# A graph attention layer with residual and layer norm: the third tile's masks put first, x loaded by rows a quad at a time, an early flag, and the moments spread between mask steps

## The chip, the cores and the metric

The kernel runs on one core of a Trainium2 chip. The metric is device time in microseconds (us) of one execution. Engines are called PE (TensorE, the matrix engine; PEld is its weight load), DVE (VectorE), ACT (ScalarE), POOL (GpSimd) and SP (SyncE, here only a DMA queue). ACT and POOL also start DMAs from their own queues.

## What is computed

```python
f1 = (w1 @ (W @ x.T)).T + b1                 # 4096 x 1
f2 = (w2 @ (W @ x.T)).T + b2
logits = f1 + f2.T                           # 4096 x 4096
bias = where(adj > 0, 0, -1e9)
coefs = softmax(leaky_relu(logits) + bias, axis=-1)
y = x + coefs @ x                            # x is 4096 x 128, float32
out = (y - mean(y)) / sqrt(var(y) + 1e-5)    # over the 128 columns
```

adj is 4096 x 4096 int32 (64 MiB), so the whole matrix has to be read once.

## The kernel before

Leaky relu has two branches, and on each the exponential of f1 + f2 is a product of a row factor and a column factor. So `coefs @ x` is, for each row tile, two sums over columns: one with the mask "edge and f1 + f2 negative" (m = 1, called minus) against a table of x scaled by exp(0.01 f2), one with the mask "edge and positive" (m = 0, plus) against a table scaled by exp(f2). The tables `btv[m]` are 32 blocks of 128 columns; each block is 258 wide: x in float16 (high part), its denominator column, and a low part that restores precision. They are built in four chunks of eight blocks (h = 0 to 3): `scale_x` (DVE) or `scale_act`/`scale_first` (ACT) multiply x by the column factor, `split_x` (ACT) writes the high part, `low_x` (DVE) the low part.

The 4096 rows are 32 tiles of 128 rows, in 8 quads of four; a quad's tile c uses buffer slot c. Per tile: SP and ACT each load half of the 2 MiB of adj (`load_tile`, `load_far`); DVE makes int8 of it (`cast`, L743); ACT writes the sign of f1 + f2 in four instructions (`signs`, L474); DVE joins the two (`combine`, L748), transposes in 32 x 32 squares (`turn`, L756) and derives the plus mask (`plus`, L761); PE does 32 matmuls for minus and 32 for plus (`edge_sums`, L1091) of 258 columns each; ACT takes both sums out of PSUM scaled by the row factors (`evacuate`). `turn` of tile t waits until PE is done with tile t-4, whose mask buffers it overwrites.

Per quad, `moments(q - 2)` on DVE adds the sums, divides, adds x from `xn`, and takes mean and variance; POOL makes the reciprocal deviation (`rows`), ACT normalises, POOL stores. It stands in one block between the second and the third tile of quad q.

Ahead of the loop is a stage written out by hand, in which each engine's order is fixed. PE transposes x block by block (`turn_x`), ACT copies that out (`xT_out`), PE multiplies it with a vector to get f1 by columns (`f1_columns`, L1047); DVE gets f2 from products and row sums (`f2_products`, L693 and L697). `spread_f1` (L710) waits for the last `f1_columns`. `stat_max`/`stat_out` bring ranges of f1 and f2 to all partitions. The first four tiles are done in this stage, with the tables growing beside them. On POOL, seven small instructions compute the row factors' exponents (`ea`, from L385) and then ten more a flag (L396 to L409) that says whether the fast path is numerically safe; SP, ACT, POOL, PE and DVE read it before the loop. ACT's first signs in the loop (tile 4) come after that read. x in row order, `xn` (2 MiB, 512 bytes a row piece), is loaded by four DMAs of 512 KiB on POOL's queue (L380), after `f1_made` and the second cast.

Of the kernel before, what the change touches and what calls it, by code (L numbers as in the profile page):

```python
# [5 lines left out]
ALU = mybir.AluOpType  # L6
# [10 lines left out]
P = 128  # L17
# [25 lines left out]
def gat_kernel(nc, x, adj, W, w1, b1, w2, b2, out):  # L43
# [24 lines left out]
    with ExitStack() as ctx:  # L68
# [14 lines left out]
        junk = sb("junk", [P, KB * D], BF16)  # L83
# [70 lines left out]
        F2_PE = (0, 2)  # L154
        F2_AT = (FIRST * KB, NK - FIRST * KB)
# [6 lines left out]
        f2_made = sem("f2_made")  # L162
# [41 lines left out]
        y_act = sem("y_act")  # L204
        y_ready = [sem(f"y_ready{m}") for m in range(2)]
# [143 lines left out]
        def _(pool):  # L349
# [25 lines left out]


            pool.wait_ge(f1_made, 2)
# [6 lines left out]
            pool.wait_ge(gst_ready, 2)  # L384
# [11 lines left out]
            pool.tensor_tensor(rng[:, 0:1], gst[:, 0:1], gst[:, 1:2], ALU.add).then_inc(rng_step, 1)  # L396
            pool.tensor_scalar(rng[:, 1:2], gst[:, 0:1], gst[:, 1:2], None, ALU.max).then_inc(rng_step, 1)
            pool.wait_ge(rng_step, 2)
            pool.tensor_tensor(rng[:, 1:2], rng[:, 1:2], gst[:, 2:3], ALU.add).then_inc(rng_step, 1)
            pool.tensor_scalar(rng[:, 0:1], rng[:, 0:1], F2_SPAN, None, ALU.is_le).then_inc(rng_step, 1)  # L400
            pool.tensor_scalar(rng[:, 2:3], gst[:, 3:4], (SCALE * X_MAX) ** 2, None, ALU.is_le).then_inc(rng_step, 1)
            pool.tensor_scalar(rng[:, 3:4], gst[:, 3:4], (SCALE * X_MIN) ** 2 * N, None, ALU.is_ge).then_inc(rng_step, 1)
            pool.wait_ge(rng_step, 6)
            pool.tensor_scalar(rng[:, 1:2], rng[:, 1:2], F_ABS, None, ALU.is_le).then_inc(rng_step, 1)
            pool.tensor_tensor(rng[:, 2:3], rng[:, 2:3], rng[:, 3:4], ALU.mult).then_inc(rng_step, 1)
            pool.wait_ge(rng_step, 8)
            pool.tensor_tensor(rng[:, 0:1], rng[:, 0:1], rng[:, 1:2], ALU.mult).then_inc(rng_step, 1)
# [39 lines left out]
            with pool.Else():  # L447
                with pool.Fori(0, NT) as t:
# [8 lines left out]
        def _(act):  # L457
# [13 lines left out]
            def signs(t, c, between=None):  # L471

                for g in range(G):
                    ins = act.activation(sgn[:, c, g * JA:(g + 1) * JA], f2b[:, :], ACT.Sign,  # L474
                                         bias=nf1l[:, bass.ds(G * t + g, 1)], scale=-1.0)
                    if g == 1 and between:
                        between()
                ins.then_inc(sign_ready, 1)
# [6 lines left out]
            def f2_copy(i):  # L485

                b = F2_PE[i]
                bank, at = (0, F2_AT[0] + b * KB) if b < FIRST else (7, F2_AT[1] + (b - FIRST) * KB)
                act.wait_ge(f1_made if b < FIRST else f2_made, 1)
                act.activation(f2l[:, b * KB:(b + 1) * KB], ps[:, bank, at:at + KB], ACT.Copy).then_inc(f2l_act, 1)  # L490

            def f2_sums(n0, n1):
                act.wait_ge(xv_ready, 3)
                for n in range(n0, n1):
# [723 lines left out]
```

## Time and profile before

| | us |
|---|---|
| median of 3 runs | 274.12 (273.82 to 276.17) |
| the profiled execution | 275.19 |
| its span, first to last instruction | 273.5 |
| TensorE's mean granted clock | 0.997 |

The profile is of one execution. Its page gives for each engine the busy time and its share of the span; the same in 40 equal slices; the DMA queues; the chain of work that ended last; and the costliest groups of instructions. From the trace come the timeline (instructions in order of time), the waits, and busy time by windows. A releaser behind `<-` is what ended an idle time.

### The profile page before, as it was taken

To read this page: it belongs to the slowest core of one execution; us is meant where nothing else is said; L and a number is where in the kernel's file an instruction comes from. 1 tells how busy PE (TensorE), PEld (TensorE's weight loads), DVE (VectorE), ACT (ScalarE), POOL (GpSimd) and SP (SyncE) were. 2 spreads that over 40 slices of the span, in tenths; PEclk is the share of its full clock that TensorE was granted. 3 is DMA by queue.
4 is the path that set the end of the run, shared out by engine and by line. 5 is a ranking of instruction groups with operands and counts; after the bars stand their busy time and mean duration, and the time that the engine had idled before them with its cause. 6 is when DMAs were issued, how large, how long until landed. Compare 5 with 4: busy or idle time off the path is not lost.

```text
span 273.5 us, 5997 instructions
## 1 busy us (share of the span) xinstructions
PE 258.2 (94%) x2195; PEld 225.6 (82%) x2195; DVE 242.6 (89%) x309; ACT 195.6 (72%) x296; POOL 67.2 (25%) x98
## 2 busy tenths in 40 slices
PE   2999988799999999999999999999999999999991
PEld 2989877688888888888888888888888888888880
DVE  2888999988888899999999999999998999999963
ACT  2479999949999996999199919991999198003140
POOL 4002046930000006300630063006300630054150
PEclk9999999999999999999999999999999999999998
DMA  6999999999999999999999999999999999801011
GB/s 196 256 298 309 311 313 282 285 272 311 313 315 318 315 314 315 323 339 315 316 324 342 318 316 280 361 328 327 240 335 309 309 285 337 226 2 38 0 49 31
DMA packets 22562, 73.64 MB, mean 269 GB/s; under 512 B 3090, under 2 KB 4244, under 8 KB 22548
## 3 DMA queue, kind: packets, MB, share of 16 engines
q1 hardware_dynamic: 11184, 35.17, 42.9%
q10 hardware_dynamic: 9956, 34.64, 42.0%
q0 software_dynamic: 1408, 3.67, 4.7%
q8 instruction: 6, 0.10, 0.2%
q14 instruction: 8, 0.07, 0.1%
HBM read 71.37 MB, written 2.10 MB: 269 GB/s over the span
## 4 chain that ended last, share of the span: by engine, by line
DVE 58%; PE 16%; issue 8%; ACT 7%; DMA 7%; DVEq 1%; ACTq 1%; POOL 1%; POOLq 0%
DVE mn L743 19%; PE ps L1091 16%; DVE msk L756 11%; DVE mn L748 11%; DMA nat<-in_adj 5%; DVE post L855 3%; ACT sgn L474 3%; DVE ybt L870 2%; DVE bns L875 2%; ACT bt L542 2%; DVE ntot L860 2%; DVE post L857 2%; ACT post L518 2%; DMA msk<-in_x 2%; DVE mv L879 1%
## 5 line engine op out<-in xcount | busy, mean ns | idle before, releaser
L1091 PE MATMUL ps<-bt,msk 128*128 128x258 f16 x2048 | 232.1, 274 | 3.6 <-DVE msk L756 2.7
L1091 PEld LDWEIGHTS ps<-bt,msk 128*128 128x128 fp8e5 x2048 | 200.5, 98 | 34.2 <-issue 4.6
L474 ACT ACTIVATE sgn<-f2b,nf1l 128x1024 int8<-128x1024 f32 x128 | 136.4, 1144 | 5.2 <-POOL flag L409 4.0
L743 DVE TENSOR_SCALAR mn<-nat 128x4096 int8<-128x4096 int32 x32 | 73.1, 2284 | 5.0 <-DMA nat<-in_adj 4.6
L416 POOL TENSOR_SCALAR nmr<-mv 128x4 f32<-128x4 f32 x7 | 12.8, 1835 | 143.5 <-DVE mv L879 143.5
L756 DVE STREAM_TRANSPOSE msk<-mn 128x1024 uint32<-128x1024 uint32 x32 | 39.8, 1245 | 2.6
L748 DVE SCALAR_TENSOR_TENSOR mn<-sgn,mn 128x1024 uint32<-128x1024 uint32 x32 | 39.2, 1225 | 3.0 <-ACT sgn L474 2.0
L623 ACT ACTIVATE ybt<-ybt,nmr,rstd 128x128 f32<-128x128 f32 x28 | 11.5, 483 | 38.7 <-POOL nmr L421 38.7
L616 ACT ACTIVATE post<-ps,ac 128x258 f32<-128x258 f32 x60 | 24.8, 467 | 10.9 <-PE ps L1091 10.9
L761 DVE TENSOR_SCALAR msk<-msk 128x1024 uint32<-128x1024 uint32 x32 | 22.2, 695 | 1.0
L427 POOL DMA_DIRECT2D out<-ybt x24 | 13.7, 572 | 16.3 <-ACT ybt L623 14.9
L1047 PEld LDWEIGHTS ps<-vsb,xn 128*128 128x128 f32 x64 | 14.3, 332 | 0.5 <-issue 0.4
L1047 PE MATMUL ps<-vsb,xn 128*128 128x1 f32 (+1 forms) x64 | 13.9, 343 | 0.0
L1034 PE MATMUL ps<-ident,msk 128*128 128x128 f32 x32 | 8.6, 430 | 2.0 <-DMA msk<-in_x 2.0
L738 DVE SCALAR_TENSOR_TENSOR bt<-bt,post 128x1024 f16<-128x1024 f16 x8 | 9.6, 1223 | 0.6 <-ACT bt L542 0.6
L870 DVE SCALAR_TENSOR_TENSOR ybt<-ntot,rec,xn 128x128 f32<-128x128 f32 x28 | 8.0, 347 | 1.8 <-DVE rec L864 1.8
L542 ACT ACTIVATE bt<-post 128x1024 f16<-128x1024 f32 x8 | 8.2, 1051 | 0.6 <-DVE post L732 0.5
L855 DVE TENSOR_TENSOR post<-post 128x1032 f32<-128x1032 f32 x7 | 8.6, 1227 | 0.0
L1034 PEld LDWEIGHTS ps<-ident,msk 128*128 128x128 f32 x32 | 6.8, 248 | 2.1 <-DMA msk<-in_x 2.1
L482 ACT ACTIVATE xn<-ps 128x512 f32<-128x512 f32 x8 | 4.7, 594 | 4.7 <-PE ps L1034 4.7
L417 POOL TENSOR_SCALAR vpe<-mv 128x4 f32<-128x4 f32 x7 | 7.6, 1081 | 0.4
L419 POOL TENSOR_TENSOR rstd<-vpe,mhalf 128x4 f32<-128x4 f32 x7 | 7.5, 1064 | 0.6
(115 smaller groups left out, 105.2 us busy)
## 6 DMA issues: line engine op xcount, KB each, us to landing
nat<-in_adj SPq DMA_DIRECT2D x64, 512.0 KB, 15.1
nat<-in_adj ACTq DMA_DIRECT2D x64, 512.0 KB, 17.6
xn<-in_x POOLq DMA_DIRECT2D x4, 512.0 KB, 19.8
out<-ybt POOLq DMA_DIRECT2D x24, 64.0 KB, 6.6
msk<-in_x SPq DMA_DIRECT2D x8, 128.0 KB, 4.2
msk<-in_x ACTq DMA_DIRECT2D x8, 128.0 KB, 4.5
out<-ybt SPq DMA_DIRECT2D x4, 64.0 KB, 1.8
out<-post SPq DMA_DIRECT2D x4, 32.0 KB, 2.4
```

Of the source, the lines that this page charges most:

```text
L427: pool.dma_start(out_g[q, g], ybt[g * SQ:(g + 1) * SQ, s]).then_inc(out_stored[s], 16)
L474: ins = act.activation(sgn[:, c, g * JA:(g + 1) * JA], f2b[:, :], ACT.Sign, bias=nf1l[:, bass.ds(G * t + g, 1)], scale=-1.0)
L542: act.activation(btv[m][:, h * CN:(h + 1) * CN, 0:D], ybuf[:, h], ACT.Copy, scale=1.0 / LOW).then_inc(hi_ready[m], 1)
L616: ins = act.activation(post[:, s, m, c, :], ps[:, 2 * c + m, 0:2 * DV], ACT.Copy, scale=ac[:, m, bass.ds(QT * q + c, 1)])
L743: dve.tensor_scalar(mn[:, c % 2], nat[:, c], 0, EDGE, ALU.is_gt, ALU.mult).then_inc(cast_done, 1)
L748: dve.scalar_tensor_tensor(out=mn_w[c % 2], in0=sgn_w[c], scalar=MINUS, in1=mn_w[c % 2], op0=ALU.bitwise_xor, op1=ALU.bitwise_and).then_in ...
L756: dve.transpose(turned[c].rearrange("p (b g s) -> p g b s", b=NB, g=G), mn_w[c % 2].rearrange("p (g b r) -> p g b r", g=G, b=NB)).then_inc ...
L761: dve.tensor_scalar(plus_w[c], turned[c], PLUS, 1, ALU.bitwise_and, ALU.logical_shift_right).then_inc(plus_ready, 1)
L855: dve.tensor_tensor(post[:, s, 0], post[:, s, 0], post[:, s, 1], ALU.add).then_inc(sums_added, 1)
L1034: ins = pe.transpose(ps[:, 4 + b % 2, k * P:(k + 1) * P], xl[:, n * D:(n + 1) * D], ident[:, :])
L1047: ins = pe.matmul(to, xT[:, n * P:(n + 1) * P], v, start=True, stop=True)
L1091: ins = pe.matmul(ps[:, 2 * c + m, 0:2 * DV], mask_f[c][m][:, n // KB, n % KB, :], btv[m][:, n, :], start=(n == 0), stop=(n == NK - 1))
```

## The change

It has these parts.

1. The head. DVE does casting, combining and turning of tile 2 before the plus table's chunks rather than after. The plus table's chunks are done in the order 1, 0, 2, 3 (`ORDER`), and PE sums tile 2's minus mask first and then plus chunks of tiles 0 to 2. Who scales x moves: DVE now does chunk 1 of the plus table and four more blocks of chunk 3 of the minus table, ACT does chunk 0 (plus) and the first half of chunk 3 (minus). f2 of blocks 8 to 11 comes from products rather than from PE. `xT_out(2)` to `xT_out(7)` move in ACT's order; the copy of the first f1 values (`nf1l`) goes from DVE to ACT; `spread_f1(0)` stands between a product and its row sum, `f2_rows` ahead of the two statistics.
2. x by rows: 32 DMAs of 64 KiB, four a quad, two quads before the loop and one quad per half turn in it, on POOL's queue, with two semaphores.
3. The flag: 7 POOL instructions instead of 10, the first three of them as soon as the ranges of f2 are there; the row exponents no longer wait for the second statistics.
4. The moments of a quad are cut into `add_sums`, `add_halves`, `invert`, `add_x`, `statistics` and `moments`, which stand between `cast`, `combine` and `turn` of the quad's four tiles. `normalise(q - 2)` comes after the second evacuation of quad q rather than `normalise(q - 1)` after the fourth.

The diff, cut to its core:

```diff
@@ POOL
+            def load_rows(q, s):
+                for g in range(G):
+                    pool.dma_start(xn[g * SQ:(g + 1) * SQ, QT * q:QT * (q + 1), :],
+                                   x_g[g][:, QT * q:QT * (q + 1)]).then_inc(xn_in[s], 16)
+            pool.wait_ge(gst_ready, 1)
+            (rng[:, 0:1], rng[:, 1:2]: three instructions, from gst 0 and 1)
             pool.wait_ge(f1_made, 2)
             pool.wait_ge(cast_done, 2)
-            for g in range(G):
-                pool.dma_start(xn[g * SQ:(g + 1) * SQ, :, :], x_g[g]).then_inc(xn_in, 16)
+            load_rows(0, 0)
+            load_rows(1, 1)
             pool.wait_ge(f1n_ready, G)
-            pool.wait_ge(gst_ready, 2)
...
                 rows(0, 0)
-                with pool.Fori(1, NQ // 2) as turn:
+                for turn in range(1, NQ // 2):
+                    load_rows(2 * turn, 0)
                     store(2 * turn - 2, 0)
                     rows(2 * turn - 1, 1)
+                    load_rows(2 * turn + 1, 1)
                     store(2 * turn - 1, 1)
                     rows(2 * turn, 0)
@@ ACT, the head after
+            xT_out(0); load_far(0, 0); xT_out(1); (copy of b12); f2_sums(1, CN)
+            load_far(1, 1); f2_copy(); f2_sums(2, 2 * CN)
+            act.wait_ge(nf1_made, 1)
+            act.activation(nf1l[:, 0:FIRST * KB], ...)
+            xT_out(2); load_far(2, 2)
             (de); scales(1, de); xT_out(3)
+            scale_first()
+            signs(0, 0, between={1: lambda: xT_out(4)}); load_far(3, 3)
+            split_x(1, 0); xT_out(5); split_x(1, 1); (be); scales(0, be)
+            xT_out(6); split_x(1, 2); load_far(QT, 0); xT_out(7); split_x(1, 3)
+            signs(1, 1); rows_out(); signs(2, 2); load_far(QT + 1, 1)
+            split_x(0, 1); scale_act(0); split_x(0, 0); load_far(QT + 2, 2)
+            signs(3, 3, between={1: lambda: split_x(0, 2), 2: lambda: split_x(0, 3)})
@@ DVE, the head after
+            scale_x(1, 0); scale_x(1, 1); stat_max(0, 0, 2); scale_x(1, 2); scale_x(1, 3, KB); stat_out(0, 0, 2)
             cast(0, 0, 0); combine(0, 0); low_x(1, 0); turn(0, 0)
+            low_x(1, 1); spread_f1(1, ...); (xt1); low_x(1, 2); low_x(1, 3)
             cast(1, 1, 0); combine(1, 1); (stat 2, 3); turn(1, 1)
+            scale_x(0, 1); stat_max(1, 2, 4)
+            cast(2, 2, 0); stat_out(1, 2, 4); combine(2, 2); turn(2, 2)
+            plus(0, 0); low_x(0, 1); plus(1, 1); scale_x(0, 2); low_x(0, 0); scale_x(0, 3)
+            plus(2, 2); low_x(0, 2); low_x(0, 3)
             cast(3, 3, 0); combine(3, 3); turn(3, 3); plus(3, 3)
@@ DVE, a quad
-                    pair(2 * q, q, 0)
-                    moments(q - 2, s)
-                    pair(2 * q + 1, q, 1)
+                    masks(q, 0, meanwhile=lambda: add_sums(q - 2, s))
+                    masks(q, 1, meanwhile=lambda: add_halves(q - 2, s))
+                    masks(q, 2, ahead=lambda: invert(q - 2), meanwhile=lambda: add_x(q - 2, s),
+                          behind=lambda: statistics(q - 2, s))
+                    masks(q, 3, ahead=lambda: moments(q - 2, s))
@@ PE
-            pe.wait_ge(den_ready[0], 1)
-            pe.wait_ge(xeps_ready, 1)
-            for h in range(BCH):
-                plus_sums(h, range(2))
             pe.wait_ge(turn_done, 3)
             edge_sums(2, 1)
-            for h in range(BCH):
-                plus_sums(h, [2])
+            pe.wait_ge(den_ready[0], 1)
+            pe.wait_ge(xeps_ready, 1)
+            plus_sums(ORDER[0], range(2)); plus_sums(ORDER[1], range(2))
+            plus_sums(ORDER[0], [2]); plus_sums(ORDER[1], [2])
+            plus_sums(ORDER[2], range(3)); plus_sums(ORDER[3], range(3))
```

Between `cast` and `combine` of a tile stands what is called `ahead`, between `combine` and `turn` what is called `meanwhile`, after `plus` what is called `behind`.

## Rows read from the trace of the kernel before

**Rows 1.** The page, part 1: busy us, share of the span, count

```profile
PE 258.2 (94%) x2195; PEld 225.6 (82%) x2195; DVE 242.6 (89%) x309; ACT 195.6 (72%) x296; POOL 67.2 (25%) x98
```

**Rows 2.** Windows, line L1091 alone: us, PE busy (x), PEld busy (x), clock, DMA share, GB/s

```profile
29.10:52.40 23.30, 17.11 (x128) 13.04 (x129) 1.00 1.03 301
52.40:267.40 215.00, 214.96 (x1920) 187.44 (x1920) 1.00 0.90 273
```

**Rows 3.** The page, part 4: the chain that ended last, shares by engine

```profile
DVE 58%; PE 16%; issue 8%; ACT 7%; DMA 7%; DVEq 1%; ACTq 1%; POOL 1%; POOLq 0%
```

**Rows 4.** Timeline of DVE: start us, us, line, operation, count, idle before

```profile
106.53 1.25 DVE L756 STREAM_TRANSPOSE msk<-mn 128x1024 uint32<-128x1024 uint32 x1
...
251.28 1.25 DVE L756 STREAM_TRANSPOSE msk<-mn 128x1024 uint32<-128x1024 uint32 x1
...
267.43 0.49 DVE L939 SCALAR_TENSOR_TENSOR post<-ps,ac,post 128x258 f32<-128x258 f32 x1 [2.14 <-PE ps L1091]
```

**Rows 5.** Timeline of PE in the head

```profile
25.14 1.09 PE L1034 MATMUL ps<-ident,msk 128*128 128x128 f32 x4
26.02 3.41 PE L1047 MATMUL ps<-vsb,xn 128*128 128x1 f32 x16
...
52.42 0.83 PE L1091 MATMUL ps<-bt,msk 128*128 128x258 f16 x6 [1.87 <-DVE msk L756]
```

**Rows 6.** Timeline of ACT and its DMA queue in the head

```profile
14.41 1.22 ACTq L280 DMA_DIRECT2D nat<-in_adj  x2
...
16.90 1.26 ACT L504 ACTIVATE post<-msk,cs 128x128 f32<-128x128 f32 x4
...
26.58 0.60 ACT L482 ACTIVATE xn<-ps 128x512 f32<-128x512 f32 x1
...
29.94 2.17 ACT L474 ACTIVATE sgn<-f2b,nf1l 128x1024 int8<-128x1024 f32 x2
...
32.02 1.04 ACT L542 ACTIVATE bt<-post 128x1024 f16<-128x1024 f32 x1
```

**Rows 7.** Timeline of DVE in the head

```profile
12.39 1.23 DVE L693 TENSOR_TENSOR sgn<-msk,vsb 128x1024 f32<-128x1024 f32 x1 [0.95 <-DMA msk<-in_x]
...
21.99 2.30 DVE L743 TENSOR_SCALAR mn<-nat 128x4096 int8<-128x4096 int32 x1 [0.58 <-DMA nat<-in_adj]
...
31.21 0.31 DVE L710 SCALAR_TENSOR_TENSOR f1s<-ps,b,same 128x96 f32<-128x96 f32 x1
31.51 2.28 DVE L743 TENSOR_SCALAR mn<-nat 128x4096 int8<-128x4096 int32 x1
...
35.25 1.23 DVE L748 SCALAR_TENSOR_TENSOR mn<-sgn,mn 128x1024 uint32<-128x1024 uint32 x1 [0.32 <-ACT sgn L474]
...
36.68 1.24 DVE L756 STREAM_TRANSPOSE msk<-mn 128x1024 uint32<-128x1024 uint32 x1
37.84 1.18 DVE L732 TENSOR_TENSOR post<-msk,cs 128x1024 f32<-128x1024 f32 x1
...
43.65 3.52 DVE L738 SCALAR_TENSOR_TENSOR bt<-bt,post 128x1024 f16<-128x1024 f16 x3 [0.65 <-ACT bt L542]
```

**Rows 8.** Waits: who waited for whom, us in total, times, longest

```profile
DVE mn L743 <- DMA nat<-in_adj: 4.6, 5, 1.1
ACT sgn L474 <- POOL flag L409: 4.0, 1, 4.0
DVE ybt L870 <- DVE rec L864: 1.8, 7, 0.4
```

**Rows 9.** Timeline of POOL

```profile
34.44 3.23 POOL L380 DMA_DIRECT2D xn<-in_x  x4 [7.15 <-DVE mn L743]
43.18 0.38 POOL L385 TENSOR_SCALAR gsum<-f1n,gst 128x32 f32<-128x32 f32 x1 [5.51 <-DVE gst L727]
...
52.49 2.75 POOL L404 TENSOR_SCALAR rng<-rng 128x1 f32<-128x1 f32 x1
...
56.89 0.30 POOL L409 TENSOR_SCALAR flag<-rng 128x1 int32<-128x1 f32 x1
```

More of the change, by code:

```diff
@@ L447, in _ @@
             with pool.Else():
+                for q in range(2, NQ):
+                    load_rows(q, q % 2)
                 with pool.Fori(0, NT) as t:
@@ L520, in scale_act, with scale_first @@
                 ins.then_inc(y_act, 1)
+            def scale_first():
+                act.wait_ge(cs_ready[1], 1)
+                for i in range(KB):
+                    n = (BCH - 1) * CN + i
+                    ins = act.activation(ybuf[:, BCH - 1, i], xl_chunk(BCH - 1)[:, i], ACT.Copy, scale=cs[:, 1, n:n + 1])
+                ins.then_inc(y1_act, 1)
             def rows_out():
@@ L560, in _ @@
             xT_out(3)
-            scale_first(3 * CN, 3 * CN + KB)
-            xT_out(4)
+            scale_first()
             act.wait_ge(f2b_ready, 1)
             act.wait_ge(nf1l_ready, 1)
-            signs(0, 0, between=lambda: xT_out(5))
+            signs(0, 0, between={1: lambda: xT_out(4)})
             load_far(3, 3)
             split_x(1, 0)
-            xT_out(6)
+            xT_out(5)
+            split_x(1, 1)
             act.wait_ge(nF2_ready, 1)
@@ L571, in _ @@
             scales(0, be)
-            split_x(1, 1)
+            xT_out(6)
+            split_x(1, 2)
             act.wait_ge(cast_done, 1)
@@ L801, in _ @@
             turn(0, 0)
-            scale_x(1, 2)
             low_x(1, 1)
-            low_x(1, 2)
             spread_f1(1, FIRST * KB, NK, 7, 0)
@@ L818, in _ @@
             dve.wait_ge(cs_ready[0], 1)
+            scale_x(0, 1)
+            stat_max(1, 2, 4)
+            cast(2, 2, 0)
+            stat_out(1, 2, 4)
+            combine(2, 2)
+            dve.wait_ge(y_ready[0], 1)
+            turn(2, 2)
+            plus(0, 0)
+            low_x(0, 1)
+            plus(1, 1)
             scale_x(0, 2)
-            stat_max(1, 2, 4)
+            low_x(0, 0)
             scale_x(0, 3)
-            plus(0, 0)
-            low_x(0, 0)
-            plus(1, 1)
-            stat_out(1, 2, 4)
-            low_x(0, 1)
+            dve.wait_ge(y_act, 1)
+            plus(2, 2)
             low_x(0, 2)
             low_x(0, 3)
-            cast(2, 2, 0)
-            combine(2, 2)
-            dve.wait_ge(y_act, 2)
-            turn(2, 2)
-            plus(2, 2)
             cast(3, 3, 0)
             combine(3, 3)
-            dve.wait_ge(y_ready[0], 2)
+            dve.wait_ge(y_ready[0], 3)
             turn(3, 3)
@@ L841, in _, with masks, add_sums @@
             with dve.If(go):
-                def pair(u, q, h):
-                    for t, c in [(2 * u + i, 2 * h + i) for i in range(2)]:
-                        cast(t, c, q)
-                        combine(t, c)
-                        turn(t, c)
-                        plus(t, c)
-                def moments(q, s):
+                def masks(q, c, meanwhile=None, ahead=None, behind=None):
+                    t = QT * q + c
+                    cast(t, c, q)
+                    if ahead:
+                        ahead()
+                    combine(t, c)
+                    if meanwhile:
+                        meanwhile()
+                    turn(t, c)
+                    plus(t, c)
+                    if behind:
+                        behind()
+                def add_sums(q, s):
                     if isinstance(q, int) and q == 0:
-                        dve.wait_ge(xn_in, 16 * G)
                         dve.wait_ge(xeps_ready, 1)
@@ L1154, in _ @@
             edge_sums(3, 1)
-            for h in range(BCH):
+            for h in ORDER:
                 plus_sums(h, [3])
```

230 lines of the change are left out of this document (121 added, 109 removed).

## The prediction, made before the changed kernel was run

> **What bounds the kernel.** I began with the busy shares [rows 1]: PE 94%, DVE 89%, ACT 72%. Two engines are near full, so shares alone decide nothing. The chain that ended last [rows 3] gives DVE 58% and PE 16%, which invites the reading that DVE is the bound. The windows of the mask matmuls say otherwise [rows 2]: from 52.4 to 267.4 us PE is busy for 214.96 of 215.00 us with 1920 of the 2048 matmuls, one each 0.1120 us, at a granted clock of 1.00. A tile (64 matmuls) takes 7.17 us, and PE never runs dry. The chain goes through DVE only because DVE never rests either; what tells is how far ahead it is. PE needs tile t at 52.4 + 7.17 (t - 2). Tile 10's transposed mask ends at 107.8 and PE wants it at 109.8; tile 31's ends at 252.5 and PE wants it at 260.3 [rows 4]. DVE is ahead by 2 to 8 us, always.
>
> So the end is: the moment from which PE never starves again, plus the matmuls left, plus the tail. Before, that moment is 52.42, when PE has waited for tile 2's `turn` [rows 5]; 1920 x 0.1120 = 215.0; and from DVE's last join, which waits for PE at 267.4 [rows 4], to the end of the span are 6.1 us. In the 23.3 us before that moment PE is busy with mask matmuls for 17.1 [rows 2], with 128 of them, worth 14.3 us at the full pitch. Only idle time there, and its place, can be won.
>
> **The head, step by step.** I carry the new orders through with durations from rows. The next instruction on DVE or ACT, if it doesn't depend on the one before, starts about 0.08 before that one's end (two signs take 2.17 us together [rows 6], three `low_x` 3.52 [rows 7]); if it does, about 0.1 after.
>
> *ACT.* `spread_f1(0)` now follows the last product, which ends at 13.6 [rows 7]: 0.3, PE's small matmul 0.6, and the copy `nf1l` on ACT near 14.7 to 14.8. Then `xT_out(2)` 0.6 and `load_far(2, 2)`: its two issues hold ACT's queue 1.22 us [rows 6], to 16.0. The exponent and its two copies 0.6, `xT_out(3)` 0.6, `scale_first` 1.2: 18.4. Two signs 2.1, `xT_out(4)` 0.6, two signs 2.1, `split_x` 0.95, `xT_out(5)` 0.6: 24.7. `split_x` 0.95, the second exponent with its copies 0.7, `xT_out(6)` 0.6, `split_x` 0.95: 27.85, and `xT_out(7)` ends at 28.5. In the kernel before that copy started at 26.6 [rows 6]; ten instructions have been moved ahead of it.
>
> *PE.* From `xT_out(5)` at 24.8 on: columns 1.64, transposes 0.9, columns 1.64 and 1.74 more (the pair took 3.41 [rows 5]), each behind the one before: the last `f1_columns` end near 30.8, against 29.4.
>
> *DVE.* `cast(0)` starts at 22.0 as before (adj arrives then [rows 7]), `combine` 1.15, `low_x` 1.14, `turn` 1.16, `low_x` 1.2: 29.0. Then `spread_f1(1)` needs those columns: a new wait of 1.9 us, with the whole of DVE's order behind it. From 30.9: 0.3 (with `xt1`), two `low_x` 2.3, `cast(1)` 2.33, `combine` 1.15, two statistics 0.29, `turn(1)` 1.16, `scale_x` 1.11, `stat_max` 0.44, `cast(2)` 2.2, `stat_out` 0.2, `combine` 1.31, `turn(2)` 1.25 [rows 7]: 44.9, and PE starts tile 2 at 45.05. DVE's added work (half a product 0.5, `scale_x` of plus chunk 1 1.1, four blocks of minus chunk 3 0.6; ACT gives up about as much) lies within this sum or under the wait for adj.
>
> *PE after it.* At 45.05 PE has done 64 matmuls, so 1984 are left, 222.2 us: the end of matmuls is 267.2. Before, it was 267.4. **The third tile comes 7.4 us earlier and is worth 0.2 us**, because 64 plus matmuls that used to be done before it now come behind it. That is the core of the forecast.
>
> It holds if PE finds all else in time. DVE goes on from 44.8 with `plus` 0.6, `low_x`, `scale_x`: PE wants plus chunk 1 at 48.6, ready 47.2; chunk 0 at 50.4, ready 49.5; tile 2's plus mask at 52.2, ready 51.2; chunk 2 at 54.0, ready 52.4; chunk 3 at 56.7, ready 53.5; tile 3 at 59.4, its `turn` ends 58.3; tile 4 at 66.6, ready 64.3; tile 5 at 73.7, ready 69.8. The least margin is 0.9 us; beyond it a delay passes on one for one.
>
> **The rest.** *The flag.* ACT's idle 4.0 us before tile 4's signs [rows 8] goes: it would now start them at 54.0. What is late next is ACT's own earlier work. Worth to PE: nothing, since it didn't starve there before [rows 2]. POOL: eight loads from 35.9 at 0.81 each (3.23 for four [rows 9], the upper bound as each is an eighth in size) to 42.4; then 11 small instructions where 17 took 14.0 us (43.18 to 57.19 [rows 9]), so 9.1, and 14.0 at worst: the flag falls between 51.5 and 56.4. Tile 4's signs start 1.0 after it and take 4.3, `combine` and `turn` 2.6, PE's start 0.1, so it decides from 58.6 on.
>
> *x by rows.* The same 2 MiB, of which 0.5 now compete early. Of DVE's five waits on adj, 4.6 us, all but the 0.58 of tile 0 [rows 7, 8] should vanish: 1.5 MiB less lies before the next tiles' adj, some 5 us at 301 GB/s [rows 2]. 28 more issues at 0.55 to 0.81 are 15 to 23 us of POOL, 25% busy [rows 1]; queued behind them are stores and `rows`, needed tens of us later. Cost nothing; if that cover were gone, a load of 3.2 us before `rows` delays only a normalisation.
>
> *The moments.* The same instructions. Their waits on DVE's own results, the largest group 1.8 us over seven quads [rows 8], are hidden by mask work, and the block is spread. Tile 10's margin grows from 2.0 us. PE gains nothing from it. `add_sums` now asks for the sums of a tile that is at least five behind, so it should not wait. ACT's `normalise` has the same work; the tail keeps its 6.1 us, since DVE waits for PE before the last join.
>
> **Sum.** 45.05 + 222.2 + 6.1 = 273.3 against a span of 273.5. The profiled execution took 275.19 in all, 1.1 above the median of 274.12; I take 0.2 off the median: **273.9 us**, its own range 273.2 to 274.8.
>
> A rule that speaks against part 2: the Trainium skill, page "SBUF — State Buffer", section "SBUF: two separate sides", says that a DMA on GpSimd's queue can't have its descriptors written while VectorE holds the shared port pair, about 3.1 us for one that takes 0.62 alone. By that figure the eight loads would take 24.8 us, an estimate from that page, and the flag would fall near 70. The trace agrees for POOL's arithmetic, on one element a partition: L404 took 2.75 us across `cast(3)` [rows 9]; for loads it shows 0.81, but none of those lay under a cast.
>
> **Rivals.**
> 1. *DVE is the bound, as the chain reads.* For it: 58% [rows 3] and no rest. Then 4.6 - 0.6 of DMA waits go, so 270.1. Against: PE's 0.04 us of idle in 215. Chance 0.07.
> 2. *The new wait at `spread_f1` doesn't arise*, because ACT or PE gets the columns done sooner. Then tile 2 starts up to 1.9 earlier, and chunks keep pace: 272.0. Chance 0.14, of which 0.03 beyond 1% with the noise.
> 3. *Slower: the head slips.* One of the margins of 0.9 is missed, or ACT's moved copies come later still; at 2 us beyond my sum 275.9, and slower by over 1% from 2.9 us on. Chance 0.12, 0.05 of it beyond 1%.
> 4. *Slower: POOL's queue.* Each early load is held under DVE's work as L404 was, 2.75 us: 8 x 2.75 = 22.0, to 57.9, plus 9.1 and 8.0, so tile 4 at 75.0 where PE wants it at 66.6: 8.4 lost, 282.3. For it: the one 2.75 row. Against: the loads' 0.81, and at most two casts in that stretch. Chance 0.07.
> 5. *The masks or flag don't come earlier at all.* The orders are fixed, so no; it is inside 3.
>
> The forecast itself has 0.60. Within 1% (2.7 us, about what a measurement of this kernel can tell from no change): 0.60 + 0.11 + 0.07 = 0.78. Faster by over 1%: 0.07 + 0.03 = 0.10. Slower: 0.05 + 0.07 = 0.12. The range leaves out rivals 1 and 4 and the far ends of 2 and 3: 271.8 to 276.4.
>
> **What the profile after would show.** Right: PE starts tile 2 near 45 with 64 mask matmuls behind it, and none of its time after that is idle; `spread_f1` for the second part idles about 1.9 us for PE; the flag before 56.4; no DVE wait on adj but tile 0's; eight early POOL loads at 0.6 to 0.8 each; 6.1 us from the last join to the end. Wrong: a PE idle between 46 and 67 (which release ends it tells whether 3 or 4), a pitch other than 0.112 us, or matmuls ending before 265.

## The result, and the profile after

| us | before | after |
|---|---|---|
| median (19 executions each, same chip) | 274.59 | 276.42 |
| lowest and highest | 273.59 to 276.52 | 275.94 to 282.38 |
| the profiled execution | 275.19 | 276.12 |
| its span | 273.5 | 274.0 |

The ratio after to before is 1.0073, with a 95% interval of 1.0054 to 1.0092. It leaves out executions more than 1.5% above the fastest of the same kernel (here the one of 282.38); the medians are of all. The change costs 1.8 us by the medians, 0.7%. That is less than 1%, but it is clear of the noise, it goes the other way than the forecast of 273.9, and it lies just outside the range's upper end of 276.4.

First the busy shares, the shares of the chain that ended last, GpSimd's DMA queue, and one group of POOL's work, all from the page of the kernel after (a group: line, engine, operation | busy, mean ns | idle before, what ended it; the queue: packets, MB, share):

```profile
PE 258.9 (95%) x2195; PEld 227.2 (83%) x2195; DVE 239.3 (87%) x310; ACT 194.5 (71%) x292; POOL 93.0 (34%) x123
...
q0 software_dynamic: 1856, 3.67, 4.6%
...
PE 87%; ACT 3%; DVE 3%; issue 3%; DMA 1%; ACTq 1%; POOL 1%; DVEq 0%; POOLq 0%
...
L377 POOL DMA_DIRECT2D xn<-in_x x32 | 20.2, 640 | 7.5 <-DVE mn L751 7.5
```

PE is as busy as before [rows 1]. The chain went through DVE for 58% and PE for 16% before [rows 3]; now PE has 87% of it, though nothing about what bounds the loop has changed: the same 0.112 us a matmul, the same PE that never rests. POOL is busy for 25.8 us more [rows 1]. 17.0 of them are the loads of x (20.2 us instead of the 3.23 of [rows 9]), the rest is mostly in its stores (19.0 us instead of 13.7) and small instructions that took longer.

Second, PE's timeline in the head (start us, us, line, operation, count, idle before), and the windows of the mask matmuls' line from tile 2 on (us, PE busy (x), PEld busy (x), clock, DMA share, GB/s):

```profile
40.39 1.96 PE L1131 MATMUL ps<-bt,msk 128*128 128x258 f16 x16
43.94 222.12 PE L1131 MATMUL ps<-bt,msk 128*128 128x258 f16 x1984 [1.59 <-DVE msk L764]
```
```profile
43.94:266.10 222.16, 222.12 (x1984) 193.67 (x1984) 1.00 0.88 274
```

Tile 2 starts at 43.94 instead of 52.42 [rows 5], with 1984 matmuls left instead of 1920 [rows 2], and they run as one row without a gap. The matmuls end at 266.06, against 267.39 before. So PE finished 1.3 us *earlier* in a kernel that is slower. Most or all of the 1.3 is a matter of when the inputs arrived in these two executions. DVE's first product, the first instruction that needs x, and for the kernel after also `cast(0)`, the first that needs adj, are here (the kernel before, then the kernel after):

```profile
6.44 0.69 DVE L693 TENSOR_TENSOR sgn<-msk,vsb 128x512 f32<-128x512 f32 x1 [1.73 <-DMA msk<-in_x]
```
```profile
5.55 0.69 DVE L698 TENSOR_TENSOR sgn<-msk,vsb 128x512 f32<-128x512 f32 x1 [0.96 <-DMA msk<-in_x]
...
20.67 2.28 DVE L751 TENSOR_SCALAR mn<-nat 128x4096 int8<-128x4096 int32 x1
```

Counted from x's arrival, 0.9 us earlier here, the new head has gained 0.4 us. Counted from the start of `cast(0)`, 1.3 us earlier here (21.99 before [rows 7]), it has gained nothing: from there to the last matmul are 245.40 us in both. Two profiles can't say which is the fair count, so the head's own gain lies between 0 and 0.4 us. The loss must lie behind the last matmul. These are the last rows of the timeline, of before and then of after:

```profile
267.43 0.49 DVE L939 SCALAR_TENSOR_TENSOR post<-ps,ac,post 128x258 f32<-128x258 f32 x1 [2.14 <-PE ps L1091]
...
269.64 0.57 POOL L438 TENSOR_TENSOR own<-own,mhalf 128x1 f32<-128x1 f32 x1 [3.88 <-DVE own L922]
270.24 0.35 DVE L962 TENSOR_SCALAR post<-post,mv,own 128x128 f32<-128x128 f32 x1 [0.68 <-POOL own L438]
270.62 0.85 ACTq L284 DMA_DIRECT2D out<-post  x2
```
```profile
266.10 0.48 DVE L973 SCALAR_TENSOR_TENSOR post<-ps,ac,post 128x258 f32<-128x258 f32 x1 [2.78 <-PE ps L1131]
...
268.32 0.56 POOL L444 TENSOR_TENSOR own<-own,mhalf 128x1 f32<-128x1 f32 x1 [6.09 <-DVE own L956]
268.92 0.35 DVE L1002 TENSOR_SCALAR post<-post,mv,own 128x128 f32<-128x128 f32 x1 [0.68 <-POOL own L444]
269.29 0.85 ACTq L282 DMA_DIRECT2D out<-post  x2
```

The steps are the same, at the same distances: from the join to the last store's issue 3.19 us in both. But the span ends at 273.47 before, 2.00 us after that last issue (its row ends at 271.47), and at 273.95 after, 3.81 us after it (270.14). No row of busy time stands in that stretch. It holds the closing instructions, which the views leave out and which were read from the trace's own records: each engine ends with a DRAIN, and the last semaphore steps of all engines, 0.22 to 0.26 us in all thirteen traces, come behind the later of two things, SP's closing DRAIN (it follows the landing of the last stores) and the end of GpSimd's. The column "after PE" is the distance from the last matmul's end.

```
kernel   POOL DMAs  last matmul  GpSimd DRAIN          SP's DRAIN         span
                    ends         starts   us   ends    starts  after PE   ends
before      30      267.39       269.76  2.99  272.75  273.21    5.82     273.47
after       58      266.06       268.46  5.25  273.71  271.89    5.83     273.95
```

Before, GpSimd's DRAIN was over 0.46 us ahead of SP. After, it is 2.26 us longer and sticks out by 1.82 us. That is the tail's growth from 6.1 to 7.9 us. The experiments ask what sets that length.

### The profile page after: what moved, and what is told of

The parts are those of the page before. It is cut to its first block, busy times and chain, and to the rows that moved or that the text cites. A ratio compares the mean times of both kernels' runs of the same rounds, so it can differ in the third digit from the quotient of the medians.

```text
span 274.0 us, 5941 instructions
## 1 busy us (share of the span) xinstructions
PE 258.9 (95%) x2195; PEld 227.2 (83%) x2195; DVE 239.3 (87%) x310; ACT 194.5 (71%) x292; POOL 93.0 (34%) x123
## 4 chain that ended last, share of the span: by engine, by line
PE 87%; ACT 3%; DVE 3%; issue 3%; DMA 1%; ACTq 1%; POOL 1%; DVEq 0%; POOLq 0%
PE ps L1131 80%; PE ps L1088 3%; PE ps L1075 2%; ACT sgn L482 1%; PE ps L1143 1%; DMA msk<-in_x 1%; DVE mn L751 1%; ACT xn L490 1%; ACTq L278 1%; DVE msk L764 0%; DVE mn L756 0%; ACT post L527 0%; POOL own L444 0%; ACT bt L550 0%; ACTq L466 0%
## 5 line engine op out<-in xcount | busy, mean ns | idle before, releaser
L420 POOL TENSOR_SCALAR nmr<-mv 128x4 f32<-128x4 f32 x7 | 6.2, 888 | 106.2 <-DVE mv L911 106.1
L431 POOL DMA_DIRECT2D out<-ybt x24 | 19.0, 798 | 32.5 <-ACT ybt L627 32.5
L377 POOL DMA_DIRECT2D xn<-in_x x32 | 20.2, 640 | 7.5 <-DVE mn L751 7.5
L425 POOL TENSOR_TENSOR nmr<-nmr,rstd 128x4 f32<-128x4 f32 x7 | 12.0, 1713 | 0.5
L423 POOL TENSOR_TENSOR rstd<-vpe,mhalf 128x4 f32<-128x4 f32 x7 | 10.5, 1501 | 0.6
```

Of the source, the lines that this page charges most:

```text
L377: pool.dma_start(xn[g * SQ:(g + 1) * SQ, QT * q:QT * (q + 1), :], x_g[g][:, QT * q:QT * (q + 1)]).then_inc(xn_in[s], 16)
L425: pool.tensor_tensor(nmr[:, s], nmr[:, s], rstd[:, s], ALU.mult).then_inc(rstd_ready, 1)
L431: pool.dma_start(out_g[q, g], ybt[g * SQ:(g + 1) * SQ, s]).then_inc(out_stored[s], 16)
```

## The experiments

Four kernels ran on one chip (before's median there 274.31), four on a second (274.85), three on a third (274.50). In each, n is the number of executions behind the median.

### x by four DMAs again

The kernel after, with part 2 alone undone.

```diff
-            load_rows(0, 0)
-            load_rows(1, 1)
+            for g in range(G):
+                pool.dma_start(xn[g * SQ:(g + 1) * SQ, :, :], x_g[g]).then_inc(xn_in[0], 16)
...
-                    load_rows(2 * turn, 0)
-                    load_rows(2 * turn + 1, 1)
```

> The changed kernel with x in row order loaded again by four DMAs of 512 KiB at the old place on GpSimd's queue; POOL's loop stays written out. Theory (drain): in the profile after, all engines wait at the end for GpSimd's closing DRAIN, 5.25 us instead of 2.99, with 58 DMAs issued by GpSimd instead of 30, so 0.081 us for each more. Here 30 DMAs, so the drain takes 3.0 us and ends before SP: the span falls by 1.8 us, to 272.1 against 274.0, and the ratio to the kernel before is about 0.996. Rival A (the written-out loop fetches code late): drain and time stay as after, 276.4. Rival B (contention of adj with x): the tail stays 7.9 us, the matmuls end later than 266.1.

Measured: 274.46 us (n = 12), ratio 0.9999 (0.9972 to 1.0026). The loss is gone, and no gain shows: what is left of the change is worth less than about 0.8 us either way. GpSimd's DRAIN took 2.96 us, as before, and the span ended 6.07 us after the last matmul, so both rivals are out: the written-out loop is still there and costs nothing, and the tail didn't stay at 7.9. (The matmuls did end late, at 268.00; the clock, below, made 1.5 us of that.) The expected ratio of 0.996 was too good by 0.4%, about 1 us. The profiled execution, span 274.1, had another oddity. Windows of all engines over its head (PE busy, PEld, DVE, ACT, POOL, then clock, DMA share, GB/s):

```profile
40.00:44.30 4.30, 2.06 (x18) 1.56 (x18) 4.16 (x5) 4.09 (x10) 3.96 (x8) 0.99 1.03 284
44.30:48.00 3.70, 3.67 (x20) 2.68 (x20) 3.70 (x5) 2.53 (x3) 3.60 (x2) 0.56 1.03 283
48.00:52.00 4.00, 4.00 (x38) 3.51 (x36) 4.00 (x5) 3.83 (x5) 3.79 (x3) 1.00 1.02 291
```

PE had waited 2.27 us for tile 2's mask, and then for some 3.4 us the granted clock was at the lower level, 1.2 GHz: 20 matmuls where 37 fitted in as much time after. Its 1984 matmuls took 223.67 us instead of 222.12, so 1.5 us of this one execution are the clock's.

### The kernel before, with x by rows

Part 2 done alone.

```diff
-            for g in range(G):
-                pool.dma_start(xn[g * SQ:(g + 1) * SQ, :, :], x_g[g]).then_inc(xn_in, 16)
+            load_rows(0, 0)
+            load_rows(1, 1)
...
+                    load_rows(2 * turn, 0)
+                    load_rows(2 * turn + 1, 1)
```

> The kernel before with only the loads of x by rows, 32 of 64 KiB on GpSimd's queue (its loop written out as after). Drain theory: DRAIN 5.2 us from about 269.8, so it ends near 275.0 where the span before was 273.5: 1.7 to 2.2 us slower than before, ratio 1.006 to 1.008. Rival (the loads cost nothing and the head of the changed kernel is what is slower): ratio 1.000.

Measured: 276.96 us (n = 6), ratio 1.0104 (1.0046 to 1.0161). Part 2 alone makes the kernel before slower by 2.65 us by the medians (1.3 to 4.4 by the interval), no less than what the whole change does. DRAIN took 5.26 us. PE's timeline:

```profile
51.02 214.96 PE L1102 MATMUL ps<-bt,msk 128*128 128x258 f16 x1920 [1.88 <-DVE msk L765]
```

This row is also the fairest test of the forecast's core. Here x arrived at 5.65, in after at 5.55; the matmuls end at 265.98 here and at 266.06 there. The third tile 7 us earlier moved PE's end by nothing. The run doesn't isolate the DRAIN, though: in its profiled execution SP was late too, since its four normalised stores took 3.21 us to issue instead of 1.79 and the last ones queued behind them. SP ended 7.57 us after PE instead of 5.8, and only 0.23 us of the DRAIN stuck out.

### x by rows on SP's queue

```diff
-                    pool.dma_start(xn[g * SQ:(g + 1) * SQ, QT * q:QT * (q + 1), :],
+                    sp.dma_start(xn[g * SQ:(g + 1) * SQ, QT * q:QT * (q + 1), :],
...
+                if c == 1:
+                    sp.wait_ge(f1_made, 2)
+                    load_rows(0, xn_in[0])
+                    load_rows(1, xn_in[1])
```

The other 24 stand behind the adj loads of quads 2 and 3, 12 each.

> The changed kernel with the same 32 loads of 64 KiB issued from SP's queue instead. Drain theory: GpSimd has 26 DMAs, DRAIN about 2.7 us, hidden behind SP's end; time as with four loads, ratio about 0.996. Rival (small loads as such, their number or their contention with adj, cost the time): as the changed kernel, 1.007. SP's 28 more issues of 0.57 us could delay adj, 16 us over the run in which SP has room; if they do, DVE waits on adj.

Measured: 298.88 us (n = 6), ratio 1.0895 (1.0836 to 1.0954). The DRAIN behaved: 26 DMAs are left to GpSimd, it took 2.65 us and was hidden. The rest is a miss by 26 us. A group of the page, and SP's timeline:

```profile
L752 DVE TENSOR_SCALAR mn<-nat 128x4096 int8<-128x4096 int32 x32 | 73.2, 2286 | 36.6 <-DMA nat<-in_adj 36.2
```
```profile
35.85 9.38 SPq L304 DMA_DIRECT2D xn<-in_x  x8
45.34 32.90 SPq L278 DMA_DIRECT2D nat<-in_adj  x12
78.29 27.10 SPq L304 DMA_DIRECT2D xn<-in_x  x12
```

A load of 64 KiB held SP's queue for 1.17 us (9.38 / 8) in the head and for 2.26 us (27.10 / 12) in the loop, with adj already queued ahead of it, against 0.64 on GpSimd's. The block of twelve keeps the next adj load back by 27 us, where DVE is at most 8 us ahead of PE. DVE waited 36.2 us for adj, and PE stood still for 12.04 and 6.99 us; around each of these the granted clock was at the lower level, for 13.7 and 6.8 us. GpSimd's queue is the right one here, in spite of the DRAIN. The Trainium skill, page "DMA: Bandwidth & Descriptors", section "Issuing engine by pattern", gives simple loads to SyncE. The trace doesn't agree for this kernel, where SP's queue is the one that feeds the loop: 8.9% slower.

### 64 DMAs of 32 KiB, and 16 of 128 KiB

The same 2 MiB in other numbers of pieces; the edit is the slice in `load_rows`.

```diff
-                    pool.dma_start(xn[g * SQ:(g + 1) * SQ, QT * q:QT * (q + 1), :],
+                    for i in range(2):
+                        at = QT * q + i * QT // 2
+                        pool.dma_start(xn[g * SQ:(g + 1) * SQ, at:at + QT // 2, :],
```

> The changed kernel with 64 loads of 32 KiB on GpSimd's queue, so 90 DMAs there instead of 58. Drain theory: 32 x 0.081 = 2.6 us more, DRAIN 7.8 us, time 279.0, ratio 1.016. Rival A and B: the same bytes and code in the same place, time within 0.5 us of 276.4.

Measured: 280.15 us (n = 7), ratio 1.0170 (1.0121 to 1.0219). With 90 DMAs on GpSimd the DRAIN took 7.55 us, to 280.23, 3.7 us past SP's end at 276.52. The DRAIN's length is as expected, but it is only a part of what this profiled execution lost (282.27 us, itself 2.1 above the median). Its span is 6.5 us longer than after's. The longer DRAIN is 2.30 of them. The last matmul came 1.84 later, of which 0.97 through the flag and 0.71 through a later start of tile 2. And the tail began late: DVE's last join started 2.11 us after the last matmul instead of waiting for it, so the DRAIN started 4.77 us after it instead of 2.40 and SP ended 8.62 after it instead of 5.83. DVE had waited 15.6 us for adj here, in 17 waits, against 2.5 in after; whether the smaller loads caused that wasn't tested. PE's timeline, then POOL's:

```profile
44.65 21.64 PE L1133 MATMUL ps<-bt,msk 128*128 128x258 f16 x192 [2.27 <-DVE msk L766]
67.26 200.64 PE L1133 MATMUL ps<-bt,msk 128*128 128x258 f16 x1792 [0.97 <-DVE msk L766]
```
```profile
36.02 10.91 POOL L379 DMA_DIRECT2D xn<-in_x  x16 [7.46 <-DVE mn L753]
...
58.97 0.29 POOL L415 TENSOR_SCALAR flag<-rng 128x1 int32<-128x1 f32 x1
```

Sixteen early loads bring the flag to 59.3 (58.97 + 0.29), and PE idles 0.97 us for tile 4. The prediction put the point from which the flag decides at 58.6; the excess of 0.7 arrives at PE as 0.97.

```diff
-                    pool.dma_start(xn[g * SQ:(g + 1) * SQ, QT * q:QT * (q + 1), :],
-                                   x_g[g][:, QT * q:QT * (q + 1)]).then_inc(xn_in[s], 16)
+                    pool.dma_start(xn[g * SQ:(g + 1) * SQ, QT * q:QT * (q + 2), :],
+                                   x_g[g][:, QT * q:QT * (q + 2)]).then_inc(xn_in[s], 16)
```

> The changed kernel with x in 16 loads of 128 KiB on GpSimd's queue, so 42 DMAs there. So far the closing DRAIN took 2.65 us with 26 DMAs, 2.96 to 2.99 with 30, 5.25 with 58 and 7.55 with 90. Drain theory: 2.98 + 12 x 0.081 = 3.95 us, which ends about 0.5 us after SP, so the median lies 0.3 to 0.6 above that with four loads (274.46): 274.9. If the kind of the loads and not the number of DMAs set it, the drain would be nearer 3 or 5.

Measured: 274.72 us (n = 12), ratio 1.0006 (0.9984 to 1.0028). With 42 DMAs the DRAIN took 3.95 us and ended at 272.54, 0.52 us past SP. From 58 to 42 DMAs, with not a byte less, nearly all the loss is gone.

### 28 DMAs of four bytes

The kernel before, with 28 DMAs of 4 bytes each on GpSimd's queue after `rows(0, 0)`. It tells the count from the bytes.

```diff
                 rows(0, 0)
+                for i in range(28):
+                    pool.dma_start(tiny[0:1, i:i + 1], b1.partition_broadcast(1)).then_inc(tiny_in, 16)
+                pool.wait_ge(tiny_in, 16 * 28)
```

> The kernel before with 28 more DMAs of 4 bytes each on GpSimd's queue, written into a tile that nothing reads, so 58 DMAs there as in the changed kernel, but hardly a byte more. It leaves nothing out. Drain theory by number: DRAIN 5.25 us, ratio 1.007. Rival (bytes, rows or descriptors set the drain): DRAIN 3.0 us, ratio 1.000.

Measured: 280.55 us (n = 6), ratio 1.0210 (1.0158 to 1.0263). The DRAIN took 5.28 us with 58 DMAs, as in after: its length goes with the count, not with the bytes. The time is three times as far above before as expected (1.021 instead of 1.007), and no clean price of a DRAIN. Only 1.64 us of the DRAIN stuck out past SP. DVE's last join started 2.41 us after the last matmul, so the DRAIN started 4.74 us after it and SP ended 8.38 after it. All 28 DMAs stand in one block, and GpSimd's stores and `rows` behind it; that this delay made the tail late is likely, not shown:

```profile
106.36 20.09 POOL L433 DMA_DIRECT2D tiny<-in_L_gnn_b  x28
136.12 2.47 POOL L429 DMA_DIRECT2D out<-ybt  x4 [9.66 <-issue]
```

The thirteen traces together. The packets are those of GpSimd's queue, from part 3 of the pages:

```
DMAs issued   packets   closing DRAIN, us
26               832    2.65  (x on SP's queue)
30              1408    2.96 to 2.99  (before and six others)
42              1600    3.95
58              1856    5.25 (after), 5.26 (before with x by rows)
58              2304    5.28 (four-byte DMAs)
90              2880    7.55
```

That is 0.07 to 0.08 us for each DMA on top of some 0.6, wherever in the kernel it was issued; the last x load in after was issued at 242.6, 26 us before the DRAIN began. The packets, a rival to the count, are out: 448 more of them at the same count change nothing (5.26 and 5.28), and 576 more between 26 and 30 DMAs cost no more than the four DMAs do (0.32 us). Where the DRAIN starts 2.4 us behind the last matmul and SP ends 5.8 behind it, as in before and after, it sticks out from 3.4 us on, about 36 DMAs. The kernel before had 30.

### Earlier column copies

The head's new wait, 2.04 us at `spread_f1`, stems from ACT's copies of x, of which ten instructions had been put ahead of the last. This kernel is the one with four x loads, with `xT_out(2)` ahead of the wait for f1, `load_far(2, 2)` behind `scale_first`, and the rest one place earlier each.

```diff
+            xT_out(2)
             act.wait_ge(nf1_made, 1)
...
-            xT_out(2)
-            load_far(2, 2)
...
-            signs(0, 0, between={1: lambda: xT_out(4)})
+            load_far(2, 2)
+            signs(0, 0, between={1: lambda: xT_out(4), 2: lambda: xT_out(5)})
...
-            xT_out(5)
+            xT_out(6)
             split_x(1, 1)
...
-            xT_out(6)
+            xT_out(7)
             split_x(1, 2)
```

> The version with four loads, and ACT's copies of transposed x earlier: xT_out(2) before the wait for the first f1 rows, load_far(2, 2) behind scale_first, xT_out(5) between the last two signs of tile 0, xT_out(6) and (7) one split earlier each. Theory: VectorE's wait of 2.04 us at the second spread_f1 is for these columns; the last of them ends at 28.7 instead of 29.6, tile 2's matmuls start 0.9 earlier, and the time falls by 0.9 us, ratio 0.997 (1984 matmuls still behind it). Rival: the signs and splits put back are what bounds the head, and the time stays as with four loads, 274.46.

Measured: 272.67 us (n = 12), ratio 0.9919 (0.9890 to 0.9947). The same kernel on the third chip, with two variants beside it:

> The same kernel as e6_columns (four loads of x, transposed x copied out earlier), to stand on one chip beside the next two. It measured 0.9919 of the kernel before, with half of its runs near 272.1 us and half near 274.1; expected again 0.990 to 0.994.

Measured: 272.67 us (n = 11), ratio 0.9953 (0.9932 to 0.9974). The ratio lies outside the 0.990 to 0.994 expected of the repeat, though its interval reaches into them, and the first was more than twice as far below before as its expected 0.997, so the size of the gain is known only roughly. Both say faster than before, by 1.3 to 2.2 us or 0.5 to 0.8%, and by way of before, by 1.2 to 1.5% faster than the changed kernel. DVE's and PE's rows of the second:

```profile
27.96 0.32 DVE L712 SCALAR_TENSOR_TENSOR f1s<-ps,b,same 128x96 f32<-128x96 f32 x1 [0.30 <-PE ps L1082]
```
```profile
42.11 222.12 PE L1125 MATMUL ps<-bt,msk 128*128 128x258 f16 x1984 [1.62 <-DVE msk L759]
```

The wait is 0.30 us instead of 2.04, everything behind it on DVE comes 1.7 us earlier, PE starts tile 2 at 42.11 with the same 1984 matmuls left, and they end at 264.23. Here a head is worth something, because PE starts its unbroken row earlier *without* having left work for later. DRAIN 2.97 us, hidden.

The profiled execution of the first (274.03 us, of the slower half) shows the limit. Its wait at `spread_f1` was gone too:

```profile
22.62 2.28 DVE L746 TENSOR_SCALAR mn<-nat 128x4096 int8<-128x4096 int32 x1
...
29.85 0.32 DVE L712 SCALAR_TENSOR_TENSOR f1s<-ps,b,same 128x96 f32<-128x96 f32 x1 [0.28 <-PE ps L1082]
```

But `cast(0)` started at 22.62, 1.95 us later than in after, and PE started tile 2 at 44.00, no sooner than after did. With the columns early, it is adj's arrival that sets the head.

### The head alone, the moments, and the flag

Four x loads and the new head, with the moments in one block and the old order of the flag's instructions:

```diff
-                    masks(q, 0, meanwhile=lambda: add_sums(q - 2, s))
-                    masks(q, 1, meanwhile=lambda: add_halves(q - 2, s))
...
+                    masks(q, 0)
+                    masks(q, 1)
+                    add_sums(q - 2, s)
+                    add_halves(q - 2, s)
+                    invert(q - 2)
+                    add_x(q - 2, s)
+                    statistics(q - 2, s)
+                    moments(q - 2, s)
+                    masks(q, 2)
+                    masks(q, 3)
```

> The changed kernel with four loads of x, with the old order of the flag on GpSimd and the moments of a quad in one block again: of the change only the head is left. Theory (TensorE is the bound, and neither flag nor moments lie on its path): as with four loads and all the rest, 274.46, ratio 1.000. Rival (VectorE is the bound in the loop): 1 to 4 us slower than with four loads.

Measured: 275.51 us (n = 12), ratio 1.0034 (1.0002 to 1.0065). Expected was 1.000. The interval lies just above that, but against the first experiment (0.9999, other chip) the intervals overlap, so whether anything was lost is open. PE's row is unbroken, 222.12 us from 43.57. The same two edits one by one, on the kernel with earlier copies, next to it on one chip (the moments' block is the diff above):

> e9 with the moments of a quad in one block again. If TensorE alone bounds the loop, the same time as e9 within 0.3 us. Rival: the block of 5.5 us on VectorE leaves tile 10 a margin of about 2 us, which runs with slower adj use up; then 0.5 to 1 us slower than e9, mostly in the slower runs. The head alone (e7) measured 1.0034 and the version with four loads 0.9999, on different chips, so this is open.

Measured: 273.72 us (n = 12), ratio 0.9985 (0.9952 to 1.0018), 1.05 us over its neighbour's 272.67 where at most 0.3 was expected, with intervals that just overlap. The rival's size came true, but not its mechanism, as the last stores show, of the kernel with spread moments and of this one:

```profile
258.90 1.79 SPq L318 DMA_DIRECT2D out<-ybt  x4
260.73 7.50 SPq L282 DMA_DIRECT2D out<-post  x10
...
264.26 0.48 DVE L969 SCALAR_TENSOR_TENSOR post<-ps,ac,post 128x258 f32<-128x258 f32 x1 [2.78 <-PE ps L1125]
```
```profile
262.09 1.82 SPq L318 DMA_DIRECT2D out<-ybt  x4
263.96 5.83 SPq L282 DMA_DIRECT2D out<-post  x10
264.63 0.48 DVE L974 SCALAR_TENSOR_TENSOR post<-ps,ac,post 128x258 f32<-128x258 f32 x1 [0.47 <-PE ps L1130]
```

PE's row is unbroken in both (it ends at 264.23 and 264.59). With the block DVE comes out of the loop later: it waits 0.47 us for PE's last sums instead of 2.78, the stores of the last whole quad are issued 3.2 us later, and the last tiles' stores queue behind them on SP. SP ended 6.85 us after PE instead of 5.82. In this pair the spreading is worth about 1 us, in the tail and not in the loop. It isn't lost with every block: in before DVE's last join waits 2.14 us [rows 4] and SP ends 5.82 after PE, and with the head alone 1.83 and 5.93; in the other two kernels with the block (x by rows, four-byte DMAs) the join doesn't wait for PE, and SP ends 7.57 and 8.38 after it. With spread moments the last join waits 2.78 us in seven of eight traces; the eighth is the one with 64 loads.

The flag's old order, ten instructions behind the exponents as in before, instead of seven of which three come first:

```diff
-            pool.wait_ge(gst_ready, 1)
-            pool.tensor_tensor(rng[:, 0:1], gst[:, 0:1], gst[:, 1:2], ALU.add).then_inc(rng_step, 1)
...
             pool.wait_ge(f1n_ready, G)
+            pool.wait_ge(gst_ready, 2)
...
+            pool.tensor_tensor(rng[:, 0:1], gst[:, 0:1], gst[:, 1:2], ALU.add).then_inc(rng_step, 1)
...
```

> e9 with the old order of the flag on GpSimd (ten instructions behind the row factors). If the flag is off the path: as e9 within 0.3 us. Rival: tile 4's signs, which start about 1 us after the flag, come too late for tile 4, whose margin is now smaller than before since TensorE starts its run earlier; then up to 1 us slower than e9, with an idle time of TensorE before tile 4 in the trace.

Measured: 273.52 us (n = 12), ratio 0.9966 (0.9945 to 0.9986), against 0.9953 (0.9932 to 0.9974) with the new order: not told apart. Its wait and its windows:

```profile
ACT sgn L478 <- POOL flag L413: 6.9, 1, 6.9
```
```profile
42.10:46.00 3.90, 3.87 (x22) 2.86 (x23) 3.90 (x5) 2.55 (x3) 3.82 (x5) 0.59 1.02 286
46.00:50.00 4.00, 4.00 (x38) 3.50 (x36) 4.00 (x5) 3.83 (x5) 3.83 (x3) 1.00 1.02 268
```

ACT waits 6.9 us for the flag and PE still doesn't idle before tile 4. Its matmuls took 223.63 us, the 1.5 us over 222.12 again at the lower clock level, again after PE's idle 2.27 us before tile 2.

## Why the prediction was wrong, point by point

**What bounds the kernel: right.** PE's row is unbroken from tile 2 to the end, 0.1120 us a matmul, at a clock of 1.00. The first rival, DVE as the bound, is out: the waits on adj did shrink from 4.6 to 2.5 us and no time came of it. (They didn't go as forecast: two in the loop, 1.81 and 0.71 us, were left.)

**The head: right.** The new wait at `spread_f1` was put at 1.9 us:

```profile
29.65 0.32 DVE L717 SCALAR_TENSOR_TENSOR f1s<-ps,b,same 128x96 f32<-128x96 f32 x1 [2.04 <-PE ps L1088]
```

Tile 2 was to start at 45.05 with 64 matmuls done. It started at 43.94, or 44.8 with x as late as in the profile of before. The end of the matmuls was to be 267.2; corrected the same way it was 266.95, a gain of 0.4 on before where 0.2 was forecast. Counted from `cast(0)` there was no gain; the forecast's 0.2 lies between the two. No margin was missed. The second rival needed a shorter wait, the third a late start; neither came. The earlier column copies then made the second rival's mechanism real by an edit, and paid as it said: it priced a start 1.9 us earlier at 272.0, and the kernel that starts 1.8 earlier measured 272.67, where before had 0.4 more than in the forecast's runs.

**The flag: inside the range, at its upper end.** It was to fall between 51.5 and 56.4. It came at 56.2, because the eleven small instructions took 14.4 us instead of 9.1 (the prediction had 14.0 as the worst). One of them alone took 4.31, beside two `low_x` and a cast of DVE's, and ended with the cast:

```profile
50.49 4.31 POOL L410 TENSOR_SCALAR rng<-gst,rng 128x1 f32<-128x1 f32 x1
54.91 1.28 POOL L413 TENSOR_SCALAR flag<-rng 128x1 int32<-128x1 f32 x1
```
```profile
50.22 2.35 DVE L746 SCALAR_TENSOR_TENSOR bt<-bt,post 128x1024 f16<-128x1024 f16 x2
52.49 2.28 DVE L751 TENSOR_SCALAR mn<-nat 128x4096 int8<-128x4096 int32 x1
```

ACT's idle there didn't go, as the prediction said, but grew from 4.0 us [rows 8] to 4.92, and tile 4's signs started at 57.15 instead of 54.0. That it costs PE nothing held.

**The early loads: right in the sum, but the fourth rival's mechanism is real.** Eight were to take 0.6 to 0.8 us each, the fourth rival said 2.75:

```profile
35.16 6.63 POOL L377 DMA_DIRECT2D xn<-in_x  x8 [7.47 <-DVE mn L751]
...
38.54 3.25 POOL L377 DMA_DIRECT2D xn<-in_x  x2
```
```profile
38.84 2.27 DVE L751 TENSOR_SCALAR mn<-nat 128x4096 int8<-128x4096 int32 x1
```

That is 0.83 each on average, across a `turn`, a product and a cast of DVE's, but the average hides two kinds. Seven took 0.55 to 0.67 us. The seventh in order took 2.70 (the last two are the row at 38.54) and ended at 41.25, 0.13 us behind the end of `cast(2)`. It is no exception. In the thirteen traces 60 of the 516 DMAs that POOL issued after the first 20 us took over 1 us, up to 2.70. Each of them ended 0.10 to 0.15 us behind the end of a cast, and none of the other 456 lay wholly inside a cast. What the rival had wrong is that every load would be held: a cast held one, and the rest went before or behind it, as the prediction's "at most two casts in that stretch" allows. The Trainium skill, page "SBUF — State Buffer", section "SBUF: two separate sides", has about 3.1 us for a DMA held this way. The traces agree with the mechanism, for casts, with 2.70 as the longest; they don't bear out the estimate of 24.8 us for all eight (6.63).

**The failed step: "x by rows ... Cost nothing", and with it "the tail keeps its 6.1 us".** Both sentences looked at what is queued behind the loads, the stores and `rows`, and found tens of us of cover. They didn't look at the closing DRAIN, whose length goes with the number of DMAs. The mis-sized term is the tail: 6.1 forecast, 7.9 measured, all of it in GpSimd's closing DRAIN, at 0.08 us for each of 28 more DMAs (2.26 us, of which 0.46 was slack). The trace of before held the sign: its rows stop 2.00 us short of the span's end, and the 6.1 us were carried over as one number without asking what those 2.00 us were.

**The sum as it came out.** From the forecast of 273.9 to the measured 276.42 are 2.5 us. The tail gives 1.8. The head was 0.2 better, if its gain is put at 0.4. The kernel before itself had a median of 274.59 in these runs and 274.12 in those the forecast stood on, 0.5. The rest, 0.4, lies outside the span: total time less span has a median of 1.70 us in before, 2.13 in after, 2.04 in before with x by rows, and 1.72 to 1.88 in all the other kernels. It goes with the 32 loads of 64 KiB on GpSimd's queue, but the kernels with 64 of 32 KiB (1.81) and with 28 tiny ones (1.72) don't have it, so the count doesn't explain it. **It stays open.** That the DRAIN causes the 1.8 us rests on its length following the count over five counts, on the span's end following the later of it and SP in all thirteen traces, and on the loss going with the count when the same bytes come in 4 or 16 loads; that no other cost of part 2 hides in the loop rests on after's unbroken row.

**The moments: costed right for the loop, wrong for the tail.** "PE gains nothing from it" held. But with a head that is early enough, spreading them lets DVE leave the loop ahead of PE, and saved about 1 us of stores at the end in the one pair of kernels that differ in nothing else. On the head of the change itself the runs don't tell.

## What to carry to other kernels

Before cutting a transfer into more pieces on GpSimd's queue, count the DMAs that queue issues in the whole kernel, and see how long the span goes on behind the last row: the closing DRAIN grows by 0.08 us for each, and it costs nothing only until it passes the last stores' landing. When the matrix engine runs without a gap, ask of a reordered head not what starts earlier but when the unbroken row starts and how many instructions are left in it: a tile moved ahead of work that must be done anyway is worth nothing, a removed wait ahead of the row is worth its length, until the next input's arrival sets the start. Read the longest of a group of equal DMAs beside their mean: a mean of 0.83 us hid one of 2.70, held by a cast. And a queue that feeds the loop is no place for small loads.

## What the runs showed that was not expected

- GpSimd's closing DRAIN: 2.65, 2.97, 3.95, 5.25 and 7.55 us for 26, 30, 42, 58 and 90 DMAs, whatever their bytes (4 to 512 Ki), packets and age.
- A DMA issued by POOL while DVE casts an adj tile was held until 0.10 to 0.15 us behind the cast's end: 60 cases in twelve of the thirteen traces, up to 2.70 us, against 0.5 to 0.95 otherwise.
- A load of 64 KiB in 512-byte pieces held SP's queue 1.2 to 2.3 us with adj loads queued ahead, and GpSimd's 0.64.
- After an idle of 2.27 us before tile 2, PE's clock fell to the lower level for some 3.4 us in two executions, at 1.5 us; after the same 2.27 us, or 2.28 and 2.29, it did not in four others. After 1.59 to 1.88 us it never did, in seven traces.
- A POOL instruction on one element a partition took 4.31 us beside two `low_x` and a cast of DVE's and ended with the cast, where the longest in before had been 2.75 [rows 9].
